# A two-layer Perceiver block on one core: when the expert rows of the first mixture are gathered, and when the next attention's contexts are loaded

## The reference

```
x = x + L0_xattn(norm(x), ctx)     # 16 heads over the 1024 keys
x = x + L0_attn(norm(x))           # a convolution along the sequence (S4)
x = x + L0_ffn(norm(x))            # first mixture: 16 experts, each token's best 4, weighted by a softmax
x = x + L1_xattn(norm(x), ctx)     # one head: softmax(norm(x) ctx^T / 16 + mask) ctx, then a layer norm, gamma, beta
x = x + L1_attn(norm(x))           # a state-space scan (Mamba)
x = x + L1_ffn(norm(x))            # second mixture: 8 experts, best 2, and a shared one
```

```
fused = sum over its 4 experts of w[e] * (gelu(norm(x) w1[e]^T + b1[e]) w2[e]^T + b2[e])
```

## Time and profile before

| what | us |
|---|---|
| median of 3 timed runs | 710.83 (710.42 to 714.6) |
| the profiled execution, its own time | 712.5 |
| its span, first to last instruction | 710.7 |

### The profile page before, as it was taken

The page is one execution under the profiler, slowest core; times in us unless marked ns, Lnnn a source line. Parts: engine busy times, 40 slices in busy tenths (PEclk is TensorE's granted clock), DMA queues, the critical chain, the costliest instruction groups (busy, mean ns, idle before and its releaser), DMA issues.

```text
span 710.7 us, 15537 instructions
## 1 busy us (share of the span) xinstructions
PE 676.7 (95%) x5712; PEld 554.0 (78%) x5712; DVE 543.6 (76%) x1212; ACT 414.0 (58%) x790; POOL 452.4 (64%) x487
## 2 busy tenths in 40 slices
PE   6899999999999988999999999998899899999998
PEld 3677778777777767999999999996457456666787
DVE  5887878787889776577777777754647999998676
ACT  3665656656665653566667667641336886665441
POOL 4848635546487644888998787736315699898130
PEclk9999999999999998999999999999999999999999
DMA  8301101011006565899999989975874610001000
GB/s 343 129 2 61 61 1 59 6 53 60 0 0 252 209 242 240 317 365 414 422 348 331 347 334 333 346 305 193 325 310 156 249 51 1 0 1 46 1 0 30
DMA packets 20365, 123.38 MB, mean 174 GB/s; under 512 B 2304, under 2 KB 6672, under 8 KB 13008
## 3 DMA queue, kind: packets, MB, share of 16 engines
q1 hardware_dynamic: 17376, 114.59, 42.0%
q0 software_dynamic: 2928, 8.00, 3.1%
HBM read 111.77 MB, written 10.81 MB: 172 GB/s over the span
## 4 chain that ended last, share of the span: by engine, by line
PE 81%; DVE 9%; ACT 5%; issue 3%; POOL 1%; DMA 1%; DVEq 0%; SPq 0%; ACTq 0%; PEldq 0%; POOLq 0%
PE banks L2279 70%; PE banks L2347 8%; DVE shown L2145 2%; PE banks L2911 2%; ACT probs L1155 1%; DVE negmax_raw L1674 1%; PE banks L2588 1%; ACT banks L1445 1%; DVE banks L2152 1%; DMA table<-in_table 1%; DVE xn L1566 1%; PE banks L2747 0%; ACT turned_back L1456 0%; POOL q_heads_hi L713 0%; POOL rstd L701 0%
## 5 line engine op out<-in xcount | busy, mean ns | idle before, releaser
L2279 PE MATMUL banks<-xT,raw 128*128 128x128 f32 x992 | 150.5, 275 | 0.6 <-DVE xT L1932 0.6
L2279 PEld LDWEIGHTS banks<-xT,raw 128*128 128x128 f32 x992 | 133.6, 191 | 3.1 <-issue 1.3
L971 POOL TENSOR_TENSOR w_lo<-raw,w_hi 128x1024 fp32r<-128x1024 f32 x52 | 122.8, 2389 | 0.9 <-ACT w_hi L1275 0.5
L1306 ACT ACTIVATE banks<-banks,later 128x128 f32<-128x128 f32 x208 | 70.5, 340 | 58.1 <-PE banks L2279 56.3
L1938 DVE CAST mid_hi<-banks 128x128 fp32r<-128x128 f32 x208 | 60.2, 289 | 36.5 <-ACT banks L1306 34.4
L1185 ACT ACTIVATE probsT<-banks 128x512 f32<-128x512 f32 x68 | 40.1, 598 | 74.8 <-PE banks L2347 74.5
L1055 POOL TENSOR_TENSOR inject<-BCbc,drive 128x1024 f32<-128x1024 f32 x31 | 72.8, 2362 | 11.3 <-DVE shown L2145 6.5
L1155 ACT ACTIVATE probs<-banks,negmax 128x1024 f32<-128x1024 f32 x64 | 71.2, 1113 | 11.7 <-DVE negmax L1676 9.9
L1674 DVE TENSOR_REDUCE negmax_raw<-banks 128x1 f32<-128x1024 f32 x64 | 77.5, 1211 | 0.4 <-PE banks L2279 0.3
L2279 PE MATMUL banks<-w_hi,mid_hi 128*128 128x256 f32 x208 | 75.5, 363 | 0.0
L2347 PE MATMUL banks<-table,probs 128*128 128x128 f32 x512 | 69.6, 279 | 0.4 <-DVE probsT L1647 0.4
(11 more groups left out here) (362 smaller groups left out, 1707.7 us busy)
## 6 DMA issues: line engine op xcount, KB each, us to landing
raw<-in_w SPq DMA_DIRECT2D x31, 2048.0 KB, 10.0
ctx_raw<-in_ctxT SPq DMA_DIRECT2D x8, 1024.0 KB, 4.7
ctxT<-in_ctxT SPq DMA_DIRECT2D x4, 2048.0 KB, 8.8
ctxN<-in_ctxN SPq DMA_DIRECT2D x4, 2048.0 KB, 13.9
x_slots<-zero SPq DMA_DIRECT2D x1, 3968.0 KB, 12.5
y_slots<-y_tile POOLq DMA_DIRECT2D x29, 128.0 KB, 7.0
wf<-in_w SPq DMA_DIRECT2D x9, 384.0 KB, 5.9
BCbc<-bc_rows SPq DMA_DIRECT2D x6, 512.0 KB, 6.9
```

Source lines behind the costliest of these rows:

```text
L971: nc.gpsimd.tensor_tensor(w2_lo[i % WB][:, cols], raw[i % WB][:, EW // 2:][:, cols], w2_hi[i % 2][:, cols].bitcast(F32), ALU.subtract).the ...
L1306: nc.scalar.activation(to, held, ACT.Gelu, bias=b1[:, bass.ds(at + u, 1)]).then_inc(gelu_done, 1)
L2279: return nc.tensor.matmul(o, lhsT, rhs, start=start, stop=stop)
```

## The change

On SP, T(1) now waits until chunk 0 has been gathered; T(2) and N(1) wait only for last_taken; T(1), T(2) and N(1) are each issued as four transfers of 512 KB. On POOL, the gathers of chunk 1 wait for the last gelu of the mixture, rstd_of(4, 0) comes behind them, then all gathers of chunk 2, rstd_of(4, 1), and those of chunk 3. On DVE, combine(1) moves behind add_sums and arrive(0). On PE, add_last(0) moves behind the loop, and the keep_running(4, 1) after open_scores(0) goes.

```diff
@@ -48,6 +48,7 @@
 ROWS_FROM = 4
 RANKED, LOWEST, TAKEN = 8, -3.0e38, 3.0e38
 LAST, MASK_FROM = 2, 6
+CTX_T_PARTS, CTX_N_PARTS = (1, 4, 4, 1), (1, 4, 1, 1)
 COLD = TILES - LAST
 SUM_BANKS = (2, 3)
 SPREAD_AT = tuple(UNITS * i + u for i, u in ((4, 0), (4, 4)))
@@ -597,12 +598,20 @@
                 sp.dma_start(raw[i % WB][:], of).then_inc(raw_loaded[i % WB], 16)
 
             def context_T(p):
-                sp.dma_start(ctxT2[p][:], d["ctxT"][2 * p:2 * p + 2].rearrange("b p c n -> p b c n"))\
-                    .then_inc(ctxT2_loaded[p], 16)
+                if CTX_T_PARTS[p] == 1:
+                    sp.dma_start(ctxT2[p][:], d["ctxT"][2 * p:2 * p + 2].rearrange("b p c n -> p b c n")).then_inc(ctxT2_loaded[p], 16)
+                    return
+                for b in range(2):
+                    for keys in (slice(0, KEYS // 2), slice(KEYS // 2, KEYS)):
+                        sp.dma_start(ctxT2[p][:, b, :, keys], d["ctxT"][2 * p + b][:, :, keys]).then_inc(ctxT2_loaded[p], 16)
 
             def context_N(p):
-                sp.dma_start(ctxN2[p][:], d["ctxN"][2 * p:2 * p + 2].rearrange("b p k n -> p b k n"))\
-                    .then_inc(ctxN2_loaded[p], 16)
+                if CTX_N_PARTS[p] == 1:
+                    sp.dma_start(ctxN2[p][:], d["ctxN"][2 * p:2 * p + 2].rearrange("b p k n -> p b k n")).then_inc(ctxN2_loaded[p], 16)
+                    return
+                for b in range(2):
+                    for of in (slice(0, KC // 2), slice(KC // 2, KC)):
+                        sp.dma_start(ctxN2[p][:, b, of, :], d["ctxN"][2 * p + b][:, of, :]).then_inc(ctxN2_loaded[p], 16)
 
             sp.wait_ge(pads_ready, 1)
             sp.dma_start(x_slots.rearrange("(p a) n -> p (a n)", p=P).rearrange("p (k n) -> p k n", k=8), over(zero[:], 8, 1))\
@@ -650,10 +659,10 @@
                 if i == TILES - WB + 1:
                     context_N(0)
                 if i == COLD - 1:
-                    sp.wait_ge(y_stored[i % YB], 16 * (i // YB + 1))
+                    sp.wait_ge(gathered[0], 16 * TOP0)
                     context_T(1)
 
-            sp.wait_ge(gathered[2], 16 * TOP0)
+            sp.wait_ge(last_taken, last_before + LAST)
             context_T(2)
             context_N(1)
             for k in range(YB):
@@ -1015,13 +1024,12 @@
             for k in range(YB):
                 pool.wait_ge(y_stored[k], y_stores(k))
             gather_rows(0)
+            pool.wait_ge(gelu_done, TILES * UNITS)
             gather_rows(1)
+            rstd_of(4, 0)
             pool.wait_ge(last_taken, last_before + LAST)
-            gather_rows(2, range(2))
-            rstd_of(4, 0)
-            gather_rows(2, range(2, 3))
+            gather_rows(2)
             rstd_of(4, 1)
-            gather_rows(2, range(3, TOP0))
             gather_rows(3)
             rstd_of(4, 2)
             rstd_of(4, 3)
@@ -2029,12 +2037,12 @@
                 norm_tile(5, p)
 
             combine(0)
-            combine(1)
             add_sums(0, 1)
             norm_begin(4, 0)
             add_sums(1, TC)
+            arrive(0)
+            combine(1)
             norm_begin(4, 1)
-            arrive(0)
             arrive(1)
             greatest(0)
             combine(2)
@@ -2154,7 +2162,7 @@
                     if n == 0:
                         dve.wait_ge(first_rows, 2 * GS)
                     elif m == 0 and g <= SPLIT_ROWS:
-                        dve.wait_ge(c_landed[g - 1], raw_loads(1 + g) + 32)
+                        dve.wait_ge(c_landed[g - 1], raw_loads(1 + g) + 16 * CTX_T_PARTS[g] + 16)
                     elif m == 0:
                         dve.wait_ge(rows_landed[g], 16)
                     if n >= 2:
@@ -2709,13 +2717,12 @@
                     turn_gates()
                 if i == COLD and u == UNITS - 1:
                     begin_sums()
-                if i > COLD and u == UNITS - 2:
-                    add_last(i - 1 - COLD)
                 if n + AHEAD < TILES * UNITS:
                     up(n + AHEAD)
                 down(n)
 
-            add_last(LAST - 1)
+            for k in range(LAST):
+                add_last(k)
             keep_running(4, 2)
 
             def open_scores(p):
@@ -2728,7 +2735,7 @@
 
             def score2(p):
                 k = p % 2
-                pe.wait_ge(ctxT2_loaded[p], raw_loads(p + 1) + 16)
+                pe.wait_ge(ctxT2_loaded[p], raw_loads(p + 1) + 16 * CTX_T_PARTS[p])
                 pe.wait_ge(early_ready, TC + p + 1)
                 for half in range(2):
                     for c in range(DC):
@@ -2748,7 +2755,7 @@
                     last.then_inc(turned2, 1)
 
             def mix2(p):
-                pe.wait_ge(ctxN2_loaded[p], 48 if p == TC - 1 else 32)
+                pe.wait_ge(ctxN2_loaded[p], (32 if p == TC - 1 else 16) + 16 * CTX_N_PARTS[p])
                 pe.wait_ge(left2_ready, p + 1)
                 pe.wait_ge(right2_ready, p + 1)
                 if p >= 2:
@@ -2765,7 +2772,6 @@
                 score2(p)
 
             open_scores(0)
-            keep_running(4, 1)
             turn_tokens(4, 0, EARLY_BANKS)
             score2(0)
             next_scores(1)
```

## The result

The changed kernel is slower: 1.0049 [1.0038, 1.0059] times the kernel before, 714.51 us median against 711.84 (17 runs of each). The forecast was 711.0 and no change, with a range of 707.9 to 713.8: the time lies above the range, and the interval of the ratio does not hold 1. A difference of half a per cent was thus clear of the noise, where the prediction had taken one per cent for the least that a measurement can tell. A part of the distance is the base: the prediction had three runs of the kernel before, with a median of 710.83. But 1.0049 times 710.83 is 714.3, and that lies outside the range too.

What follows compares the result with a forecast made beforehand. PE was taken to bound the kernel, with 81% of the chain. The profiled 712.5 minus 0.2 is 712.3, less 1.67 over the median 710.6, plus 0.4 for the stall's chance: 711.0 us, no change, range 707.9 to 713.8.

Steps and rivals of the forecast that it cites:

- Score 0: First score on PE, after the mixture: to start at 494.9, 3.3 us earlier than before.
- combine(1): Chunk 1's combine on DVE: to wait for its gathers until about 497.5, landing 6.53 us after issue beside the loads.
- Chunks 2 and 3 at zero: After chunk 1's scores: later or earlier gathers and loads of chunks 2 and 3 were taken to cost or gain zero.
- The gathers land as without load: Rival on chunk 1's gathers: landing 2.81 us after issue, score2(1) 2.8 us earlier, 708.4 us; chance 0.2.
- The stall stays: Rival at the mixture's end: last gelu still ends at 491.15, score2(1) 3.8 us later, 715.0 us; chance 0.12.
- a rival, with 0.15: Clock falls while PE idles 3.1 us before score2(1): half that score at 1.2 GHz costs 1.8 us, 712.8; chance 0.15.
- the prediction's own sign of being wrong: Among the signs listed as showing the forecast wrong: a PEclk of 0.50 near 500.
- I take the stall as gone: Mixture's end: PE's stall before the last down() pair, costing 1.63 us, disappears; the last gelu ends at 487.1.
- the subtraction of 1.67: Profiled execution stood 1.67 us over the median of 710.83, so its predicted 712.3 became 710.6.
- the 0.2 gained: At score2(1): start at 502.6 against 502.78 before, 0.2 us gained.
- one chance in four: Chance that the stall belongs to the profiled execution alone, costing +1.6 us; it added 0.4 to the forecast.
- Quarters don't change that: Context loads issued in quarters: chunk 1's gathers still land as late beside them, 6.53 us after issue.

Runs made afterwards that it cites:

- before_again: The kernel before, unchanged, profiled a second time; it took 710.3 us.
- early1_split: The changed kernel without the gathers' wait for the last gelu, chunk 1's rstd ahead of chunk 2's fourth gather; the mix starts 1.59 us earlier, none reaching the end.
- fill: The changed kernel with three unused matmuls on TensorE between the two scores; the mix starts 2.59 us earlier than in the changed kernel.
- late_loads: The changed kernel with T(2) and N(1) held until chunk 1's gathers have landed; ratio 1.0023 to the kernel before.
- gelu_wait: The kernel before with only the change's wait of chunk 1's gathers for the last gelu; ratio 1.0079.
- whole: The changed kernel with whole context loads in place of quarters; chunk 1's last gather lands 6.92 us after its issue, and TensorE waits 3.77 us.
- before_t1: The kernel before with only T(1) made to wait for chunk 0's gathers; TensorE idles 4.31 us before its first score, which takes 5.33 us.

## Why the prediction was wrong

**The steps that held.** Score 0 at 494.86 (494.9), combine(1) at 497.41 (497.5), an idle TensorE of 3.02 us (3.1), released by chunk 1's tokens. That combine(1) is met to 0.1 is partly luck: the gathers were issued 0.26 later than worked out and landed 0.34 sooner. Chunks 2 and 3 at zero: from the mix to the end it is 202.43 in the changed kernel and 202.38 in before_again. It holds with chunk 1 as late as here; with chunk 1 early the same stretch is 203.93 in early1_split. "The gathers land as without load" fell: 6.19, not 2.81. The Trainium skill (DMA: Bandwidth & Descriptors, section Queues, rings and completion order) says that the engines alternate between queues packet by packet. What I had read from that, that a small gather need not stand behind a large load, does not agree with 2.82 against 7.12 for the same four gathers; whether the alternation itself fails no run here shows. "The stall stays" fell as well.

**The step that failed first: the clock was left at full rate through the idle stretch** and only a rival, with 0.15, had it fall. It fell, at 503.11 - 2.45 = 500.66, where the prediction's own sign of being wrong had it (near 500). And that rival's price was too small: 1.8 stood for half of the score at the slow rate; in the trace the score took 2.20 more (5.85 - 3.65), and the tokens and the opening in front of it were slow as well (0.69 and 1.20 for 0.44 and 0.71); against fill it is 2.59 in all. The rows had a fall at 266 us, after a stretch in which TensorE was busy for 1.31 of 2.00, and no fall over the wait of 1.47, as the busy time by stretch of the kernel before has it:

```profile
490.00:492.00 2.00, 0.70 (x2) 0.30 (x2) 1.14 (x4) 0.43 (x2) 0.00 (x0) 1.00 0.09 35
```

A wait twice as long as any in the rows that kept the clock should have given the fall more than 0.15; at best the rows left it open. The Trainium skill (TensorE: Matmul & The Clock Gate, section What's actually happening) makes the slow rate the default and the fast one earned by activity. Fill agrees: matmuls without use kept PEclk at 1.00.

**The step that failed second: "I take the stall as gone" as a gain, and the subtraction of 1.67.** The stall was gone, but it had not been in the median, so it was counted twice: in the 0.2 gained beside the profile, and again in the 1.67 by which the profile stood over the median. By the rows the stall is 1.63, by the second profile 1.77. I noted that they are alike and gave it one chance in four. (That the 1.67 comes so near is partly luck: over 17 runs the median is 711.84, and the profile stands 0.66 over it.) Taken from before_again, the first score gains 1.59 (12.24 - 10.65), not 3.3, and the second score is 1.97 late, not 0.2 early.

With both put right the second score is 1.97 late and takes 2.20 longer, 4.17 in all; at the end it is 4.22 by the traces, and timed it is 0.0049, 3.5 us. In the forecast's own terms, the other three quarters of the 1.6 and the 2.6 of the clock make 711.0 + 1.2 + 2.6 = 714.8. Either alone, 712.2 or 713.6, would have stayed inside the range. Over the twelve kernels with a timed ratio, the timed difference ((ratio - 1) times 711.5) is on average 0.2 us below the trace's difference from before_again; a stall in every run of before, and in none of theirs, would make that 1.7. So it is in few of them. What held the signal back in the first profile was not found.

**"Quarters don't change that" failed** too, by 0.7 us of landing. It is hidden in the sum: the changed kernel has the quarters, and the landing was taken from chunk 3 beside whole loads.

## What to carry to other kernels

A wait that moves a small transfer behind an event also moves it under whatever load starts at that event: price it with the landing under that load, and then ask what the waiting engine's clock does, since the work behind an idle TensorE may run at half rate, as it did here. When a profile stands above the median, first ask whether the stall you mean to remove is the difference; a second profile of the kernel before answers it. And after each gain look at what comes late next (here chunk 2's rows, then chunk 3's): 1.6 us at the first mix was worth nothing until the loads and GpSimd's order were changed together.

## What was not expected of the hardware

The same kernel, profiled twice, had its last gelu 6.57 and 2.63 us behind the fourth-last one. Idle stretches of TensorE of 2.47 us (late_loads) and 3.99 (gelu_wait) went with half rate for 3.4 us, 3.02 (after), 3.77 (whole) and 4.31 (before_t1) with 6.8, and the scores behind them took 4.89 and 5.35, 5.85, 5.87 and 5.33: the cost did not follow the wait's length. The half rate near 265 us lasted between 6.83 and 13.65 us in the traces, in a stage that no edit touches, and the timed runs of one kernel spread with the granted clock: of the 29 runs of before beside fill, those at 0.995 took 710.1 to 711.8 us, those at 0.990 712.6 to 713.4.
